# A graph-convolution block on one core: the opening of the first two batches put in another order

## The reference

```python
h0 = maximum(layernorm(x), 0)                      # no gain, no bias
H  = (adj != 0)                                    # incidence, 0/1
w  = adj[0, :]                                     # edge weights: first row
Dn = 1 / (H @ w)   (0 where H @ w is 0)            # node degrees
Be = 1 / H.sum(axis=0)                             # edge counts
conv(v, W, b) = Dn * (H @ (Be * (H.T @ (v @ W.T)))) + b
z  = layernorm(relu(conv(h0, W1, b1))) * gamma + beta     # 512 wide
out = x + (conv(z, W2, b2) + h0)
```

## Time and profile before

| | us |
|---|---|
| median of 3 runs (lowest, highest) | 662.37 (661.37, 662.79) |
| the profiled execution: its time | 663.38 |
| the profiled execution: span from the first to the last instruction | 661.6 |

### The profile page before, as it was taken

The page is one execution under the profiler, slowest core; times in us unless marked ns, Lnnn a source line. Parts: engine busy times, 40 slices in busy tenths (PEclk is TensorE's granted clock), DMA queues, the critical chain, the costliest instruction groups (busy, mean ns, idle before and its releaser), DMA issues.

```text
span 661.6 us, 11883 instructions
## 1 busy us (share of the span) xinstructions
PE 623.1 (94%) x4744; PEld 467.4 (71%) x4744; DVE 490.3 (74%) x1145; ACT 290.9 (44%) x539; POOL 114.0 (17%) x137
## 2 busy tenths in 40 slices
PE   0997579999999999999999999999999999999998
PEld 0743465768858687668867688577876688586887
DVE  6879968788668966799478877599577994478632
ACT  3243483636344553536425363536435354224720
POOL 5317110401221030400303021300304012000000
PEclk9999689999999999999999999999999999999999
DMA  8992539013991079511990159700994029200801
GB/s 319 207 362 57 96 73 334 41 33 96 197 345 33 1 173 248 217 33 36 219 347 38 33 134 187 316 33 1 198 267 172 33 68 211 41 1 2 191 2 63
DMA packets 146214, 90.29 MB, mean 136 GB/s; under 512 B 134768, under 2 KB 135408, under 8 KB 141168
## 3 DMA queue, kind: packets, MB, share of 16 engines
q1 hardware_dynamic: 146160, 89.54, 49.5%
HBM read 47.58 MB, written 8.39 MB: 85 GB/s over the span
## 4 chain that ended last, share of the span: by engine, by line
PE 86%; DVE 9%; ACT 3%; DMA 1%; issue 0%; DVEq 0%; ACTq 0%
PE acc L544 17%; PE acc L561 17%; PE acc L488 15%; PE acc L525 12%; PE acc L505 11%; PE acc L468 6%; PE acc L470 6%; DVE incidence L830 1%; PE acc L420 1%; PE acc L422 1%; DVE z L892 1%; ACT z_split_ring L631 1%; ACT z L632 1%; DVE junk L839 1%; DVE stat L897 1%; DVE h_split L821 1%
## 5 line engine op out<-in xcount | busy, mean ns | idle before, releaser
L544 PE MATMUL acc<-xw_split,incidence 128*128 128x256 f16 x1024 | 113.2, 273 | 0.0
L561 PE MATMUL acc<-edge_means,incidence_t 128*128 128x256 f16 x1024 | 113.1, 273 | 0.0
L592 ACT ACTIVATE edge_means<-acc,edge_inverse 128x256 f16<-128x256 f32 x128 | 55.9, 474 | 124.4 <-PE acc L544 69.7
L468 PE MATMUL acc<-h_split,incidence 128*128 128x257 f16 x448 | 100.6, 276 | 10.1 <-DVE incidence L830 10.1
L544 PEld LDWEIGHTS acc<-xw_split,incidence 128*128 128x128 bf16 x1024 | 100.1, 98 | 13.2 <-DVE xw_split L928 0.2
L561 PEld LDWEIGHTS acc<-edge_means,incidence_t 128*128 128x128 bf16 x1024 | 100.2, 98 | 13.1
L470 PE MATMUL acc<-h_split,incidence 128*128 128x256 f16 x448 | 100.6, 276 | 0.0
L488 PE MATMUL acc<-incidence_t,edge_means 128*128 128x512 bf16 x448 | 97.8, 379 | 0.0
L525 PE MATMUL acc<-w_split,z 128*128 128x256 f16 x768 | 87.4, 275 | 5.4 <-POOL w_split L400 4.1
L525 PEld LDWEIGHTS acc<-w_split,z 128*128 128x128 f16 x768 | 75.4, 99 | 16.4 <-POOL w_split L400 4.3
L505 PE MATMUL acc<-w_split,pt_split 128*128 128x512 f16 x384 | 84.2, 379 | 2.5 <-POOL w_split L395 2.5
(11 more groups left out here) (93 smaller groups left out, 625.5 us busy)
## 6 DMA issues: line engine op xcount, KB each, us to landing
adj_in<-adj SPq DMA_DIRECT2D x32, 1024.0 KB, 10.9
out<-residual SPq DMA_DIRECT2D x32, 256.0 KB, 2.5
x_in<-x SPq DMA_DIRECT2D x7, 1024.0 KB, 5.7
edge_weights<-adj SPq DMA_DIRECT2D x8, 512.0 KB, 3.7
x_in<-x SPq DMA_DIRECT2D x2, 512.0 KB, 4.5
incidence_t<-incidence SPq DMA_TRANSPOSE x32, 4.9
z<-w1t SPq DMA_DIRECT2D x1, 512.0 KB, 4.8
xw_split<-w2t SPq DMA_DIRECT2D x1, 512.0 KB, 10.2
```

Of the source, the lines that this page charges most:

```text
L468: nc.tensor.matmul(acc[:, 0:ONE + 1], inc[:, b.slot, ct, cols], h0[:, ct, 0:ONE + 1], start=(ct == 0), stop=False)
L544: last = nc.tensor.matmul(acc[:, 0:DOUT], inc[:, b.slot, ct, P * et:P * (et + 1)], xw[:, ct, part, :], start=(ct == 0 and part == HI), sto ...
L561: last = nc.tensor.matmul(acc[:, 0:DOUT], inc_t[:, b.slot, ct, et, :], edge[:, et, part, :], start=(et == 0 and part == HI), stop=(et == T ...
L592: return nc.scalar.activation(o, i, ACT.Copy, **kw)
```

## The change

It concerns the opening alone; the steady part is as before, apart from the ring of PSUM banks, which is shifted by four places.

- SyncE: the four quarters of adj come right after x; then beta, gamma, the edge weights, W1, W2 and b2. The second batch's x is loaded between the second and the third incidence transpose, and waits for `x_added` of 8 tiles instead of `res_ready`; its adj follows the transposes. The last incidence transpose of the second batch comes between the second and the third transpose of z.
- h0 of the first batch is kept whole, in the upper half of `z` (`u_first`), instead of in the ring of two groups.
- GpSimd: nothing until all 8 incidence tiles and all 8 h0 tiles of the first batch are there; then x + h0 into `res`, one `partition_all_reduce` for both weights' maxima (instead of one each), then b2 added. For the second batch `add_h0` and `add_b2`, with the second weight's low part between them.
- TensorE: `bias_times_w2` runs between the halves of B of the first batch (bank 7) instead of after C. A of the second batch waits for one drained tile of C for each of its own.
- VectorE: the low part of the first h0 group goes ahead of the statistics of the upper half of x. Degrees of the first batch: two, then three more, then the last three, in place of four, two and two. Both weights' maxima, the beta columns and W1's factor come before the edge inverses; the third maximum and W2's factor after B's first half; the second half of `b_lo` after the second batch's incidence and low parts.
- The layer norm of the first z is made in two halves of four tiles, each with its own statistics and root; the first half's splits start before the second half's are ready.

The core of the diff (of the order of SyncE's queue only the moved lines):

```diff
-    BIAS_BANK = (2 * T + 4) % 8
+    BIAS_BANK = 7
+        u_first = z[:, T // 2:T, :].rearrange("p a (k d) -> p (a k) d", d=DIN)
@@ SyncE
-                wait_reuse(sp, res_ready, b.count(T, 0))
+                if b.offset == 1:
+                    sp.wait_ge(x_added, T)
+                else:
+                    wait_reuse(sp, res_ready, b.count(T, 0))
...
+            for q in range(QUARTERS):
+                load_adj(b0, q)
+            sp.dma_start(gb[:, 1, :], beta).then_inc(weights_loaded, 16)
+            sp.dma_start(gb[:, 0, :], gamma).then_inc(weights_loaded, 16)
+            load_edge_weights(b0)
+            sp.dma_start(w1f, w1t.rearrange("(t p) h -> p t h", p=P)).then_inc(w1_loaded, 16)
+            sp.dma_start(w2f, w2t.rearrange("(t p) o -> p t o", p=P)).then_inc(w2_loaded, 16)
...
+            load_x(nxt)
             for q in range(2, QUARTERS):
                 sp.wait_ge(inc_ready, QT * (q + 1))
-                transpose_inc(Batch(0, 0), q)
+                transpose_inc(b0, q)
+            for q in range(QUARTERS):
+                load_adj(nxt, q)
@@ GpSimd
-            first_residual(Batch(0, 0))
+            pool.wait_ge(inc_ready, T)
+            pool.wait_ge(u_ready, T)
+            for t in range(T):
+                nc.gpsimd.tensor_tensor(res[:, 0, t, :], x_in[:, t, :], u_tile(b0, t), ALU.add).then_inc(x_added, 1)
             pool.wait_ge(max_here, 1)
-            nc.gpsimd.partition_all_reduce(wall[:, 0:1], wm[:, 0:1], P, RMAX).then_inc(max_all, 1)
+            nc.gpsimd.partition_all_reduce(wall[:, 0:2], wm[:, 0:2], P, RMAX).then_inc(max_all, 1)
+            pool.wait_ge(x_added, T)
+            pool.wait_ge(b2_loaded, 16)
+            for t in range(T):
+                nc.gpsimd.tensor_tensor(res[:, 0, t, :], res[:, 0, t, :], b2_row[:, :], ALU.add).then_inc(res_ready, 1)
             pool.wait_ge(w_hi, 1)
             nc.gpsimd.tensor_tensor(w1s[:, :, LO, :], w1f, w1s[:, :, HI, :], ALU.subtract).then_inc(w_ready, 1)
-            first_residual(Batch(0, 1))
-            pool.wait_ge(max_here, 2)
-            nc.gpsimd.partition_all_reduce(wall[:, 1:2], wm[:, 1:2], P, RMAX).then_inc(max_all, 1)
+            add_h0(nxt)
             pool.wait_ge(w_hi, 2)
             nc.gpsimd.tensor_tensor(w2s[:, :, LO, :], gf, w2s[:, :, HI, :], ALU.subtract).then_inc(w_ready, 1)
+            add_b2(nxt)
@@ VectorE, after incidence(b0, 3)
-            for ct in range(4):
-                degree(b0, ct)
+            degree(b0, 0)
+            degree(b0, 1)
+            (beta columns; largest(0, w1f); largest(1, gf))
+            for ct in range(2, 5):
+                degree(b0, ct)
+            factor(0, w1_scale, 1.0 / (H0_SCALE * PT_SCALE * W_SCALE))
             for half in range(2):
                 edge_inverse(b0, half)
                 for et in range(T // 2 * half, T // 2 * (half + 1)):
                     t1_lo_part(b0, et)
+            x_stats(nxt)
+            inverse_root(x_ln, x_step, nxt, X_STEPS, 1.0)
             b_lo(b0, 0)
             b_lo(b0, 1)
+            (largest(2, bias bank); its copy; factor(1, ...))
+            incidence(nxt, 0); h0_lo(nxt, 0); h0_lo(nxt, 1)
+            degree(b0, 5) to degree(b0, 7); node_inverse(b0)
+            incidence(nxt, 1); h0_lo(nxt, 2)
+            (bw_row scaled; second_degree_factor(b0))
+            incidence(nxt, 2); h0_lo(nxt, 3)
+            b_lo(b0, 2)
+            b_lo(b0, 3)
+            drain_c(b0, 0); drain_c(b0, 1); z_stats(b0, 0); drain_c(b0, 2)
+            incidence(nxt, 3)
+            drain_c(b0, 3); z_stats(b0, 1); drain_c(b0, 4); z_stats(b0, 2); z_stats(b0, 3); drain_c(b0, 5)
+            variance(z_ln, z_stat, z_half, b0, Z_STEPS, DH, lower)
+            drain_c(b0, 6); z_stats(b0, 4)
+            inverse_root(z_ln, z_half, b0, Z_STEPS, ZN_SCALE, lower)
+            drain_c(b0, 7); z_stats(b0, 5) to z_stats(b0, 7)
+            variance(z_ln, z_stat, z_step, b0, Z_STEPS, DH, upper)
+            z_lo(b0, 0); z_lo(b0, 1)
+            inverse_root(z_ln, z_step, b0, Z_STEPS, ZN_SCALE, upper)
+            z_lo(b0, 2); z_lo(b0, 3); edge_inverse(nxt, 0); t1_lo_part(nxt, 0)
+            for t in range(T // 2, T):
+                et = t - T // 2 + 1
+                z_lo(b0, t)
+                if et == T // 2:
+                    edge_inverse(nxt, 1)
+                t1_lo_part(nxt, et)
```

More of the change, by code:

```diff
@@ L195, in hypergraph_block @@
         x_half = sem("x_half")
+        z_half = sem("z_half")
         b2_loaded = sem("b2_loaded")
@@ L346, in _ @@
+            sp.wait_ge(inc_ready, 2 * T)
+            transpose_inc(nxt, QUARTERS - 1)
+            for q in range(2, QUARTERS):
+                sp.wait_ge(zs_ready, QT * (q + 1))
+                transpose_z(b0, q)
             load_x(Batch(0, 2))
@@ L360, in _, with add_h0 @@
             nc.gpsimd.memset(h0[:, :, ONE:ONE + 1], 1.0).then_inc(ones_set, 1)
[L362 to L368, removed]
+            def add_h0(b):
@@ L369, in first_residual, with add_b2 @@
                 for t in range(T):
                     pool.wait_ge(u_ready, b.count(T, t + 1))
-                    part = res[:, b.slot, t, :]
-                    nc.gpsimd.tensor_tensor(part, part, u[:, t // GT % 2, t % GT, :], ALU.add).then_inc(x_added, 1)
+                    nc.gpsimd.tensor_tensor(x_in[:, t, :], x_in[:, t, :], u_tile(b, t), ALU.add).then_inc(x_added, 1)
                 pool.wait_ge(x_added, b.count(T, T))
[L374 to L382, removed]
+            def add_b2(b):
@@ L401, in _ @@
             for n in range(N - 2):
-                residual(Batch(0, n + 2))
+                add_h0(Batch(0, n + 2))
+                add_b2(Batch(0, n + 2))
         @block.tensor
@@ L425, in first_stage_a, with bias_times_w2 @@
                         last.then_inc(a_done, 1)
+            def bias_times_w2():
+                pe.wait_ge(beta_ready, 1)
+                pe.wait_ge(w2_loaded, 16)
+                for ht in range(HT_):
+                    last = nc.tensor.matmul(acc_ring[:, BIAS_BANK, 0:DOUT], beta_cols[:, ht, :], w2f[:, ht, :],
+                                            start=(ht == 0), stop=(ht == HT_ - 1))
+                last.then_inc(bias_done, 1)
             def first_stage_b():
@@ L443, in first_stage_b @@
                                 last.then_inc(b_done, 1)
-            def bias_times_w2():
-                pe.wait_ge(beta_ready, 1)
-                pe.wait_ge(w2_loaded, 16)
-                pe.wait_ge(c_drained, 1)
-                for ht in range(HT_):
-                    last = nc.tensor.matmul(acc_ring[:, BIAS_BANK, 0:DOUT], beta_cols[:, ht, :], w2f[:, ht, :],
-                                            start=(ht == 0), stop=(ht == HT_ - 1))
-                last.then_inc(bias_done, 1)
             def stage_a(b):
@@ L717, in _ @@
                 h0_hi_part(b0, g)
+            act.wait_ge(weights_loaded, 32)
+            act.wait_ge(w2_loaded, 16)
+            for ht in range(HT_):
+                last = copy(gf[:, ht, :], w2f[:, ht, :], scale=gb[:, 0, ht:ht + 1])
+            last.then_inc(gamma_w2, 1)
             for et in range(T):
@@ L1037, in _ @@
                     t1_lo_part(b0, et)
[L1039 to L1043 removed]
+            x_stats(nxt)
+            inverse_root(x_ln, x_step, nxt, X_STEPS, 1.0)
             b_lo(b0, 0)
             b_lo(b0, 1)
[L1046 to L1060 removed]
+            dve.wait_ge(bias_done, 1)
+            largest(2, acc_ring[:, BIAS_BANK:BIAS_BANK + 1, 0:DOUT]).then_inc(bias_step, 1)
+            V.tensor_copy(bw_row[:, :], acc_ring[:, BIAS_BANK, 0:DOUT]).then_inc(bias_read, 1)
+            dve.wait_ge(bias_step, 1)
+            V.scalar_tensor_tensor(out=wall[:, 1:2], in0=wm[:, 2:3], scalar=BIAS_ROOM, in1=wall[:, 1:2],
+                                   op0=ALU.mult, op1=ALU.max).then_inc(bias_step, 1)
+            dve.wait_ge(bias_step, 2)
+            factor(1, w2_scale, 1.0 / (ZN_SCALE * W_SCALE * XW_SCALE))
             incidence(nxt, 0)
@@ L1063, in _ @@
             h0_lo(nxt, 1)
[L1064 removed]
+            for ct in range(5, T):
+                degree(b0, ct)
+            node_inverse(b0)
             incidence(nxt, 1)
[L1066 removed]
             h0_lo(nxt, 2)
[L1068 to L1090 removed]
             dve.wait_ge(w2_scale, 5)
+            dve.wait_ge(bias_read, 1)
             V.tensor_scalar(bw_row[:, :], bw_row[:, :], wr[:, 1:2], ZN_SCALE * W_SCALE * XW_SCALE,
```

219 lines of the change are left out of this document (99 added, 120 removed).

## The result

The changed kernel takes 664.17 us (median of 7 runs, 663.22 to 664.77) where the kernel before takes 662.37; the ratio is 1.0028, 95% interval 1.0017 to 1.0039. The change makes the kernel slower by 1.8 us; 655.5 was forecast. The profiled execution took 663.64 for a span of 661.9.

A forecast was written before the change was run, and what follows sets the result against it. TensorE has no slack after 107.7 us, so only the first D stage's end could move. It was summed to 100.8, a gain of 6.9: 663.4 - 6.9 - 1.0 = 655.5 us, range 648.5 to 660.5.

The forecast's parts named there:

- VectorE's list ahead of B: Sum of VectorE's steps from 11.4 us, releasing GpSimd at 19.7, ending `factor` at 31.4 and starting B at 33.5.
- the heavier case: Rival: GpSimd's adds also hold beta copies and `factor`, 2.2 + 2.0 us more ahead of B; 659.7 us, chance 0.16.
- my 8.6: Lock ahead of C's second half: thirteen adds 7.0 us, W2's subtract 1.6; last `b_lo` at 66.8.
- forecast 34.0: Chain over VectorE and ScalarE from the last `b_lo` to D's end: 34.0 us, ending at 100.8.
- I took 1.0 off for the median: Final sum: 1.0 us subtracted because the earlier kernel's profiled execution, 663.38, stood 1.0 above its median, 662.37.
- no change: Rival: the wait in C eats all, last `b_lo` at 73.7 instead of 66.8; 662 us, chance 0.06.
- First matmul: Opening: TensorE's first matmul at 11.5 us instead of 17.1, with 5.6 taken off its path.
- stage A's end: First batch: stage A lasts 17.0 us as before and ends at 28.5.
- `degree` is locked beside adds: VectorE's `degree` loses 0.54 us per GpSimd add, taking 1.7 to 1.8 us beside adds.
- 3.4 together as charged: Lower TensorE clock after long waits: 1.7 us lost in B's first half and 1.7 charged in C.
- no wait for W2 ahead of the second maximum: Gamma*W2 ready at 23.1, wanted at 25.0, cover 1.9 us; rival of W2 landing late had chance 0.06.
- my 44.2: Time of the bias result between B's halves, from which VectorE's list ahead of C's second half was summed.

The follow-up runs named there:

- e1_no_all_reduce: The changed kernel with GpSimd's all-reduce replaced by an ordinary GpSimd copy, leaving out the maximum over partitions: 657.07 us, ratio to the kernel before 0.9922.
- e4: The changed kernel with the maximum over partitions made on VectorE and TensorE, without GpSimd's all-reduce: 658.94 us, ratio 0.9954.
- e6: The changed kernel plus one more all-reduce, of a constant, as GpSimd's first work: 664.22 us, ratio 1.0027.
- e7: The changed kernel with maxima handed on by an ordinary GpSimd copy, then an all-reduce whose result nobody reads: 659.43 us, ratio 0.9955.
- e5: The changed kernel with GpSimd's eight first-batch adds of b2 moved from behind the all-reduce to behind W2's low part: 661.63 us, ratio 0.9994.
- e9: Changed kernel, maxima via TensorE, beta copies before GpSimd's adds, b2's adds held until W1's factor, W2's low part until the last `b_lo`: 652.10 us, ratio 0.9840.
- e10: The changed kernel with W2's low part on GpSimd, and the adds behind it, held until VectorE's last `b_lo`: 661.71 us, ratio 0.9982.
- e3_beta_early: The changed kernel with only the four beta copies moved ahead of GpSimd's first add: 666.36 us, ratio 1.0070.

## Why the prediction was wrong

**The step that failed** is in "VectorE's list ahead of B": "There GpSimd is let go", and then a sum in which `factor` (0.8) follows the degrees with no wait. I counted eight adds and an all-reduce as GpSimd's work, and the all-reduce with nothing. A row that prices the way back stood in my own groups: 8.67 us of "issue" behind the first all-reduce. I took no term from it. The way in stood in no row of the kernel before as a time of its own, since GpSimd was idle there anyway. I did not ask what comes before the all-reduce in the new order, ordinary adds that end 1.0 us before the maxima are ready, nor what stands behind. Against the sum: all-reduce done 36.6, factor 37.4 instead of 31.4, B at 39.3 instead of 33.5. Of these 5.8 us, 4.5 are VectorE's wait; 1.3 are VectorE's list, longer by the locked beta copies (2.2: 2.79 for 0.6, as in the heavier case) and shorter elsewhere (0.8 of it the lock on the degrees, which met only two).

**Carried on**: the bias came at 50.0 instead of 44.2, and the last `b_lo` ended at 74.2 instead of 66.8. Of these 7.4 us, 5.8 are B's delay and 1.6 more lock than my 8.6, since the held adds of b2, W1's subtract and `add_h0` left GpSimd no gap there: two `h0_lo` took 3.74. D ended at 107.85 instead of 100.8. The tail from the last `b_lo` was 33.7, forecast 34.0. Of the 8.7 us by which the median missed, 7.1 are this, and 1.5 that I took 1.0 off for the median while the changed kernel's profile lay 0.5 below its own. None of my rivals had this mechanism: "heavier" was right on the copies, and not borne out on `factor`'s steps (ahead of B they met no add; W2's took 0.13 to 0.16 each from 50.9 to 51.7, beside adds, where a locked eight-column step took 0.65), and "no change" was near in time by the wait in C, but put the cause in the lock alone.

**What held.** First matmul 11.8 (11.5); stage A's end 27.9 (28.5); the last incidence tile at 19.9 (19.7); `degree` is locked beside adds (1.78 and 1.63, free 1.21), the first maximum, beside adds all along, is not (1.21; the second, 1.20, met hardly any); the clock cost 1.9 in B's first half (8.97 against 7.07 in its second) and 1.5 in the second half of C (6.84 against 5.35), both at a granted clock of 0.78 behind the two waits, 3.4 together as charged; no wait for W2 ahead of the second maximum, none ahead of the second A. And the sum without the change-over was near: e1_no_all_reduce, where the rest of the change stands, gave 657.07. Part of that is luck: there the bias came at 46.84, 2.6 later than my 44.2, and the list behind it took 21.0 us instead of 22.6. So is stage A's end: it began 0.3 late and took 16.1 instead of 17.0.

**Shown and open.** That the all-reduce's change-over turned a gain into a loss is shown by e1, e4, e6 and e7; that GpSimd's instructions beside VectorE's list in C cost time at the end, by e5, e9 and e10 (2.5 of 3.4 us read off the rows in e10, 3.7 of 5.2 in e9). What the engine does in the 8.8 and 11.4 us no row shows beyond the MODIFY_POOL_CONFIG at their start. Not tried: the all-reduce ahead of the adds in the new order, which would delay the second x behind them.

## What to carry to other kernels

Before an instruction of another kind is moved on GpSimd, read what the profile has as "issue" on both sides of it, and ask whether the engine was idle there for another reason: hidden in the old order, it is the path in the new one. A passage that lies wholly under another wait has no row of its own; look then for what the engine's sequencer did at the start of that idle time. Where two engines take turns, count the delay on both, and count it on the engine that is waited for; putting four copies and eight adds where neither meets the other was worth 3.1 us here, and holding GpSimd off a list on the path another 3.7.

## What the hardware showed

The passage from ordinary GpSimd instructions to the all-reduce took 7.2 to 9.7 us and the way back 7.2 to 12.4, wherever the profile shows them as "issue" (seven ways in, in six kernels; in the kernel before the way in lay under a wait). Each way began with a pair of MODIFY_POOL_CONFIG. The Trainium skill (GPSIMD Engine Reference, 2.1 Instruction dispatch) says that the first call to a freshly loaded kernel pays a load of about 6 us. The traces agree that there is such a stretch, measure it longer (8.8 where the adds end just ahead), and have it again on the second all-reduce (8.83 in e6_early_all_reduce).

A copy of one column spread over 128x128 was held by GpSimd's adds (0.73 to 0.76 beside them in the changed kernel, 0.22 without them in e3_beta_early), though it reads one tensor. And the turns are not always one for one: in e3_beta_early's profile a VectorE step of 0.18 us lasted 5.96, through the end of b2's adds, a subtract and the four adds behind it, and ended as they ended (59.6).
